# Products of a recommendation tower: one sample on each quarter of the array instead of two on each half

## The chip, the cores and the metric

The kernel runs on one core of a Trainium2 chip. Five engines work side by side, each on its own list of instructions, and wait for each other by semaphores: TensorE (PE: matmuls, with the weight loads, PEld, beside them), VectorE (DVE), ScalarE (ACT), GpSimd (POOL) and SyncE (SP, which here only issues DMAs). Operands lie in SBUF (128 partitions), matmul results in PSUM. The time is that of one execution on the device, in microseconds (us).

## The reference, cut to what matters

```
e = stack([tbl_t[ids[:, t]] for t in range(26)], axis=1)      # 2048 samples, 26 embeddings of 128
combined = concatenate([e, dense[:, None, :]], axis=1)        # 27 features of 128 per sample
interact = einsum('bfd,bgd->bfg', combined, combined)         # 27 x 27 products per sample
z = interact[:, triu_i, triu_j]                               # the 351 pairs above the diagonal
h = concatenate([z, dense], axis=1)                           # 479
h = maximum(h @ W_top1 + b_top1, 0)                           # 512
h = maximum(h @ W_top2 + b_top2, 0)                           # 256
y = h @ W_top3                                                # 1
```

Everything is fp32. Ten of the tables have 1000 rows, the others 1250 to 125000.

## The kernel before

The 2048 samples go through in 8 units of 256. In each unit:

- POOL gathers rows of 16 tables by indirect DMA, one table for 128 samples at a time: 32 gathers (L402), in 8 banks of four. The place `emb` exists once, so a bank's gathers of the next unit may begin when PE has transposed the present ones. PE transposes a bank (L426, four matmuls with the identity) and ACT copies it to `feat` (L588).
- The ten tables of 1000 rows ("held") stay in SBUF, split in a high and a low part (`held_h`, `held_l`). Their rows are picked by matmuls: DVE compares the ids of 256 samples, which a DMA has spread over all partitions (`ids_row`), with row numbers and so makes a one-hot matrix `hot` (L689, two halves of 128 x 1024 per table); PE multiplies it with the table (L440 and L441, 16 matmuls per table). `hot` has two places, so the one-hot of a table waits until the table two before it has been used. `ids_row` has ten.
- PE multiplies each sample's 27 features with each other (L458). Two samples stand side by side as 54 columns, both as weights and as what streams past them, and the result is 54 x 54, of which the two blocks of 27 x 27 on the diagonal are of use. The left half of the array (result rows 0 to 53) has one pair of samples, the right half (rows 64 to 117) the next. A batch is 8 such groups of four samples, 432 columns in a bank of PSUM; a unit has 8 batches. ACT copies each to `gram` (L603).
- SP stores `gram` to DRAM (four DMAs, L323) and, when they have landed, loads the 351 pairs from there in the layout of a matmul operand (15 DMAs, L329). ACT and DVE split them in `z_h` and `z_l`.
- The layers of the unit before (L476 first, L510 and L515 second, L525 the last) are put between the tables and the products of the present one.

The order of the work is a list of steps that all engines walk through (`steps`, L89): each kind of step has a span of the unit, and `merged` sorts them by place. First the four row banks of samples 0 to 127 among the ten tables, then the other four row banks among the first half of the products, then the second half of the products. The first layer of the unit before stands at about 0.62 of the tables' part.

At the start the ids of all gathers are loaded by the ACT queue (L641), before the first two tables; SP loads ids and tables 2 to 9 at the same time. After the last unit's products come the stores, the loads of pairs, and the layers of the last unit.

Of the kernel before, what the change touches and what calls it, by code (L numbers as in the profile page):

```python
# [30 lines left out]
def dlrm_tower_kernel(nc, x_t, ids_g, ids_h, gathered, held, w1, b1, w2, b2, w3, out):  # L31
# [16 lines left out]
    S = 4  # L48
    SIDES = 2
    PAIR = S // SIDES  # L50
# [4 lines left out]
    BANK = 512  # L55
    GB = 8
    BATCHES = UC // S // GB
# [11 lines left out]
    PC = HC // PIECES  # L69
    SLOTS = NH  # L70
    PER_ROW = 2
    AHEAD = 2
    BANKS = [(f, min(4, NG - f)) for f in range(0, NG, 4)]
# [15 lines left out]
    def steps(later, last=False):  # L89
        rows = [("rows", w) for w in range(UNIT * NB)]  # L90
        tables = [("held", o) for o in range(NH)]
        gram = [("gram", b) for b in range(BATCHES)]
        z = [("z", c) for c in range(ZC)] if later else []
        l1 = [("l1", n) for n in range(1 if last else N1)] if later else []
        l2 = [("l2", n) for n in range(N2)] + [("weigh", 0)] if later and not last else []
        l3 = [("l3", 0)] if later and not last else []
        following = [("next hot", (o, q)) for o in range(2) for q in range(PIECES)]

        found = []
        for step in merged((rows[:NB], 0.05, 0.8), (tables, 0, 1), ([("dense", 0)], 0.6, 0.8), (z, 0.58, 0.64),  # L100
                           (l1, 0.9 if last else 0.62, 1)):
# [3 lines left out]
        found += merged((rows[NB:], 0, 1), (gram[:HALF], 0.1, 1), (l2, 0, 0.7), (following[:PIECES], 0, 1))  # L105
        return found + [("parts", 0)] + merged((gram[HALF:], 0, 1), (l3, 0, 0.1), (following[PIECES:], 0, 1))

# [25 lines left out]
    with ctx:  # L133
# [38 lines left out]
        for name, shape, dt in (("z_raw", [ZR, ZC, UC], fp32), ("z_h", [ZR, ZC, UC], f32r), ("z_l", [ZR, ZC, UC], f32r),  # L172
# [3 lines left out]
            late_at += 4 * math.prod(shape[1:])  # L176
        assert late_at <= placed_at["hot"] + 4 * 2 * HC * UC
        held_h = sb("held_h", [HR, NH, HC, D], f32r)
# [31 lines left out]

        ids_in = sem("ids_in")
        rows_in = [[sem(f"rows_in{h}_{w}") for w in range(NB)] for h in range(UNIT)]
        ids_row_in = [sem(f"ids_row_in{p}") for p in range(NH // PER_ROW)]
        dense_in = sem("dense_in")
# [119 lines left out]
        def _(sp):  # L334
# [13 lines left out]
            def load_ids_rows(i, p):  # L348
                reached(sp, hot_made, ((i - 1) * NH + (p + 1) * PER_ROW) * PIECES)
                sp.dma_start(ids_row[:, p * PER_ROW:(p + 1) * PER_ROW, :].rearrange("q o b -> q (o b)"),  # L350
                             ids_h[i:i + 1, p * PER_ROW * UC:(p + 1) * PER_ROW * UC].to_broadcast([128, PER_ROW * UC])
                             ).then_inc(ids_row_in[p], 16)
# [12 lines left out]
            def store_y(j):  # L365
                sp.wait_ge(y_made, j + 1)
                sp.dma_start(out[:, j * UC:(j + 1) * UC], y_of(j)[:]).then_inc(y_out, 16)

            load_ids_rows(0, 0)
            for o in range(AHEAD, NH):  # L370
                if o % PER_ROW == 0:
                    load_ids_rows(0, o // PER_ROW)
                load_table(sp, o)
            load_dense(0)
            for i in range(UNITS):
                if i == 0:
                    weights()
                if not is_last(i):
                    for p in range(NH // PER_ROW):
# [10 lines left out]
        def _(pool):  # L390
# [16 lines left out]

            pool.wait_ge(ids_in, 16)
            for i in range(UNITS):
                gather(i)  # L410

        @block.tensor
        def _(pe):
# [16 lines left out]
            def table(i, o):  # L430
# [6 lines left out]
                for c in range(HC):  # L437
                    if c % PC == 0:
                        pe.wait_ge(hot_made, n * PIECES + c // PC + 1)
                    nc.tensor.matmul(dst, held_h[:, o, c, :], hot[:, n % 2, c, :], start=c == 0, stop=False)  # L440
                    ins = nc.tensor.matmul(dst, held_l[:, o, c, :], hot[:, n % 2, c, :], start=False, stop=c == HC - 1)  # L441
                ins.then_inc(hot_used, 1)
# [123 lines left out]
        def _(act):  # L566
# [56 lines left out]
            def unit(i):  # L623
                for kind, k in steps(i > 0, is_last(i)):
# [9 lines left out]
                    elif kind == "parts":  # L634
                        dense_part(i)
                    elif kind in ("z", "l1", "l2"):
                        later(i - 1, kind, k)
                    elif kind == "hot" and k[1] == 0 and i == 0 and k[0] + 1 < NH:
                        table_high(k[0] + 1)

            act.dma_start(idx[:], ids_g[:, :, :]).then_inc(ids_in, 16)  # L641
# [4 lines left out]
            for o in range(3):  # L646
                table_high(o)
# [20 lines left out]
        def _(dve):  # L668
# [14 lines left out]
            def one_hot(i, o, q):  # L683
                n = i * NH + o
                if q == 0:
                    dve.wait_ge(ids_row_in[o // PER_ROW], 16 * (i + 1))
                    reached(dve, hot_used, n - 1)
                chunks = slice(q * PC, (q + 1) * PC)
                nc.vector.tensor_tensor(hot[:, n % 2, chunks, :],  # L689
                                        bass.AP(ids_row, (n % SLOTS) * UC, [[SLOTS * UC, HR], [0, PC], [1, UC]]),  # L690
                                        row_nums[:, chunks].unsqueeze(2).to_broadcast([HR, PC, UC]),
                                        ALU.is_equal).then_inc(hot_made, 1)
# [63 lines left out]
            def unit(i):  # L756
                for kind, k in steps(i > 0, is_last(i)):
                    if kind == "hot":
                        if i == 0 and k[1] == 0:
                            table_low(k[0])  # L760
                        one_hot(i, *k)
                        if i == 1 and k[1] == PIECES - 1 and k[0] - 2 < NW:
                            weights_low(k[0] - 2)
                    elif kind == "next hot":
# [13 lines left out]
            dve.wait_ge(rows_numbered, 1)  # L778
            for o in range(2):
                for q in range(PIECES):  # L780
# [66 lines left out]
```

## Time and profile before

| | |
|---|---|
| median of 3 runs | 375.73 us (374.99 to 376.73) |
| profiled execution | 375.79 us |
| its span, first to last instruction | 373.8 us |
| mean granted clock of TensorE | 0.977 |
| busy: PE / PEld / DVE / ACT / POOL | 333.4 / 315.3 / 247.8 / 203.4 / 252.8 us |
| products (L458): matmuls in the trace | 2048 |
| HBM read / written | 38.07 / 6.20 MB |

A busy PE is not a PE at its peak: matmuls overlap, so their cost is read from the distance of their starts. The program's fp32 matmuls appear as two each in the trace. Idle time before an instruction is put down to whoever released it. A granted clock of 1.00 is 2.4 GHz, 0.50 is 1.2 GHz.

### The profile page before, as it was taken

The numbers are of one execution on the slowest core, as the hardware profiler recorded it, in microseconds if no ns is written. First come the engines' busy times: TensorE is split into PE (matmuls) and PEld (weight loads), VectorE is DVE, ScalarE is ACT, GpSimd is POOL, SyncE is SP. The second block draws the span as 40 slices with busy tenths as digits, with TensorE's granted clock in tenths as the row PEclk, the third lists the DMA queues.
The fourth block names the chain that finished last, engine by engine and source line by source line (L and its number), as shares of the span: only waits on it lengthen the run. The fifth ranks groups of instructions, "written<-read, shape, count | busy, mean of one in ns | idle before, by whom it ended". The sixth has DMA issues, their size and how long they took to land.

```text
span 373.8 us, 9779 instructions
## 1 busy us (share of the span) xinstructions
PE 333.4 (89%) x4178; PEld 315.3 (84%) x4178; DVE 247.8 (66%) x298; ACT 203.4 (54%) x274; POOL 252.8 (68%) x262
## 2 busy tenths in 40 slices
PE   0768759969999899989999999989998999989967
PEld 0768649869899898989899998989898989988955
DVE  3999805994469835895389735995389645980324
ACT  1575475425756448536755456645855466548322
POOL 3888777877777777777777777777777777760000
PEclk9998979989999999999999999999999999999989
DMA  7995324453154532563254623563255524420310
GB/s 238 392 322 166 97 59 132 107 156 84 51 131 121 162 81 69 155 184 85 53 155 100 175 63 91 143 180 80 56 155 147 136 51 119 113 72 2 87 39 0
DMA packets 32377, 44.92 MB, mean 120 GB/s; under 512 B 18791, under 2 KB 20463, under 8 KB 32334
## 3 DMA queue, kind: packets, MB, share of 16 engines
q1 hardware_dynamic: 23080, 25.82, 24.0%
q0 software_dynamic: 8192, 16.79, 17.6%
q10 hardware_dynamic: 1062, 1.69, 1.4%
q8 instruction: 33, 0.54, 0.6%
q14 instruction: 10, 0.08, 0.1%
HBM read 38.07 MB, written 6.20 MB: 118 GB/s over the span
## 4 chain that ended last, share of the span: by engine, by line
PE 49%; DVE 21%; POOL 10%; issue 8%; DMA 6%; SPq 3%; ACT 2%; ACTq 0%; DVEq 0%
DVE hot L689 18%; PE ps_gram L458 14%; POOL emb L402 10%; PE ps_mix L476 10%; PE ps_feat L440 7%; PE ps_feat L441 7%; PE ps_feat L426 4%; PE ps_mix L510 3%; DMA products_dram<-gram 3%; SPq L329 3%; ACT feat L588 1%; DMA idx<-in_ids 1%; PE ps_mix L515 1%; PE ps_feat L476 1%; PE ps_mix L525 1%
## 5 line engine op out<-in xcount | busy, mean ns | idle before, releaser
L402 POOL DMA_INDIRECT emb<-in_tbl,idx x256 | 252.1, 985 | 81.7 <-issue 76.8
L689 DVE TENSOR_TENSOR hot<-ids_row,ps_rows 128x1024 fp32r<-128x1024 int32 x160 | 186.2, 1215 | 19.1 <-PE ps_feat L441 16.1
L440 PE MATMUL ps_feat<-hot,held_h 128*128 128x256 f32 x640 | 164.8, 295 | 15.5 <-DVE held_l L675 11.7
L588 ACT COPY feat<-ps_feat 128x512 f32<-128x512 f32 x104 | 125.7, 1229 | 76.6 <-PE ps_feat L426 44.5
L441 PE MATMUL ps_feat<-hot,held_l 128*128 128x256 f32 x640 | 159.6, 287 | 0.0
L440 PEld LDWEIGHTS ps_feat<-hot,held_h 128*128 128x128 f32 x640 | 125.0, 195 | 17.8 <-issue 14.8
L441 PEld LDWEIGHTS ps_feat<-hot,held_l 128*128 128x128 f32 x640 | 125.2, 196 | 0.0
L458 PEld LDWEIGHTS ps_gram<-feat 128*54 128x54 f32 x2048 | 56.0, 132 | 9.7 <-issue 5.4
L458 PE MATMUL ps_gram<-feat 128*54 128x54 f32 x2048 | 61.0, 217 | 1.3 <-ACT feat L588 1.3
L426 PE MATMUL ps_feat<-ident,emb 128*128 128x128 f32 x256 | 40.8, 283 | 9.0 <-DMA emb<-in_tbl,idx 9.0
L603 ACT COPY gram<-ps_gram 119x432 f32<-119x432 f32 x64 | 35.2, 550 | 9.6 <-PE ps_gram L458 9.5
L615 ACT ACTIVATE h_h<-ps_mix,b_sb 128x256 fp32r<-128x256 f32 x28 | 13.3, 474 | 49.8 <-DVE h_x L742 49.7
L426 PEld LDWEIGHTS ps_feat<-ident,emb 128*128 128x128 f32 x256 | 29.6, 143 | 10.8 <-issue 9.5
L742 DVE TENSOR_SCALAR h_x<-ps_mix,b_sb 128x256 f32<-128x256 f32 x28 | 13.5, 483 | 32.4 <-PE ps_mix L476 32.4
L476 PE MATMUL ps_mix<-z_h,w1z_h 117*128 117x256 f32 x84 | 24.2, 288 | 5.1 <-DVE z_l L734 5.1
L704 DVE TENSOR_TENSOR den_l<-dense,den_h 128x256 fp32r<-128x256 f32 x7 | 4.5, 639 | 31.4 <-ACT den_h L595 31.4
L476 PE MATMUL ps_mix<-z_l,w1z_h 117*128 117x256 f32 x84 | 23.8, 284 | 0.0
L476 PE MATMUL ps_mix<-z_h,w1z_l 117*128 117x256 f32 x84 | 23.6, 281 | 0.0
L476 PEld LDWEIGHTS ps_mix<-z_h,w1z_h 117*128 117x128 f32 x84 | 15.9, 189 | 6.1 <-DVE z_l L734 6.1
L476 PEld LDWEIGHTS ps_mix<-z_h,w1z_l 117*128 117x128 f32 x84 | 16.1, 191 | 0.0
L476 PEld LDWEIGHTS ps_mix<-z_l,w1z_h 117*128 117x128 f32 x84 | 15.9, 190 | 0.0
L510 PE MATMUL ps_mix<-h_h,w_h 128*128 128x256 f32 x45 | 14.0, 311 | 1.4 <-DVE h_l L727 1.4
(101 smaller groups left out, 248.4 us busy)
## 6 DMA issues: line engine op xcount, KB each, us to landing
ids_row<-in_ids_h SPq DMA_DIRECT2D x40, 256.0 KB, 3.9
products_dram<-gram SPq DMA_DIRECT2D x30, 189.0 KB
held_raw<-in_held SPq DMA_DIRECT2D x8, 512.0 KB, 13.1
emb<-in_tbl,idx POOLq DMA_INDIRECT x256
z_raw<-products_dram SPq DMA_DIRECT2D x84, 26.0 KB
held_raw<-in_held ACTq DMA_DIRECT2D x2, 512.0 KB, 9.2
dense<-in_dense_t SPq DMA_DIRECT2D x8, 128.0 KB
w1z_raw<-in_W_top SPq DMA_DIRECT2D x3, 234.0 KB
```

Of the source, the lines that this page charges most:

```text
L402: pool.indirect_dma_start(emb[:, h, f, :], None, table, bass.IndirectOffsetOnAxis(ap=idx[:, i * UNIT + h, f:f + 1].bitcast(u32), axis=0),) ...
L426: ins = nc.tensor.transpose(ps_feat[:, slot_of(i, ("rows", k)), f * TILE:(f + 1) * TILE], emb[:, h, first + f, :], ident[:])
L440: nc.tensor.matmul(dst, held_h[:, o, c, :], hot[:, n % 2, c, :], start=c == 0, stop=False)
L441: ins = nc.tensor.matmul(dst, held_l[:, o, c, :], hot[:, n % 2, c, :], start=False, stop=c == HC - 1)
L458: ins = nc.tensor.matmul(ps_gram[side * SIDE:side * SIDE + M, nth % GRING, g * M:(g + 1) * M], two, two, start=True, stop=True)
L476: ins = nc.tensor.matmul(bank_of(j, "l1", k), *term, start=c == 0 and m == 0, stop=c == ZC and m == 2)
L510: nc.tensor.matmul(bank_of(j, "l2", k), *term, start=c == 0 and m == 0, stop=False)
L588: nc.scalar.copy(feat_v[:, f, b], src).then_inc(act_out, 1)
L603: nc.scalar.copy(*products_copy(i, b)).then_inc(gram_act, 1)
L615: nc.scalar.activation(h1_h[:, k, :], bank_of(j, kind, k), ACT.Relu, bias=b1_sb[:, k:k + 1]).then_inc(h1_high, 1)
L689: nc.vector.tensor_tensor(hot[:, n % 2, chunks, :], bass.AP(ids_row, (n % SLOTS) * UC, [[SLOTS * UC, HR], [0, PC], [1, UC]]), row_nums[:, ...
L742: nc.vector.tensor_scalar(h1_x[:, k % 2, :], bank_of(j, kind, k), b1_sb[:, k:k + 1], 0.0, ALU.add, ALU.max).then_inc(h1_full, 1)
```

## The change

Three things are changed together.

**Products.** `SIDES` goes from 2 to 4: a matmul has one sample, 27 columns, and writes 27 rows of PSUM from partition 0, 32, 64 or 96 on. There are twice as many. A batch has 16 groups of four samples (`GB`), still 432 columns, so a unit has four batches. `gram` needs 27 x 64 numbers per partition in place of 54 x 64.

**One-hots and ids.** In the room freed, `hot` has three places (`HOTS`); the next unit's first three one-hots are made beside the products, not two. `ids_row` has places for four pairs of tables in place of five, taken in turn; the fifth pair of the next unit is loaded after the stores of the products.

**Start.** The ids for unit 0's gathers are loaded alone, as SP's first DMA; POOL waits for them, and for the others before unit 1. SP waits for table 0 before it issues further loads.

```
-    SIDES = 2
+    SIDES = 4
-    GB = 8
+    GB = 16
-    SLOTS = NH
     PER_ROW = 2
+    ROW_SLOTS = 4
+    HOTS = 3
...
-        following = [("next hot", (o, q)) for o in range(2) for q in range(PIECES)]
+        following = [("next hot", (o, q)) for o in range(HOTS) for q in range(PIECES)]
...
-            if step[0] == "held" and step[1] + 2 < NH:
-                found += [("hot", (step[1] + 2, q)) for q in range(PIECES)]
+            if step[0] == "held" and step[1] + HOTS < NH:
+                found += [("hot", (step[1] + HOTS, q)) for q in range(PIECES)]
...
-        ids_row = sb("ids_row", [128, SLOTS, UC], i32)
-        hot = sb("hot", [HR, 2, HC, UC], f32r)
+        ids_row = sb("ids_row", [128, ROW_SLOTS * PER_ROW, UC], i32)
+        hot = sb("hot", [HR, HOTS, HC, UC], f32r)
...
             def load_ids_rows(i, p):
-                reached(sp, hot_made, ((i - 1) * NH + (p + 1) * PER_ROW) * PIECES)
+                nth = i * (NH // PER_ROW) + p
+                reached(sp, hot_made, (nth - ROW_SLOTS + 1) * PER_ROW * PIECES)
...
+                    for p in range(ROW_SLOTS, NH // PER_ROW):
+                        load_ids_rows(i + 1, p)
                     reached(sp, l2_done, i * N2)
...
+            sp.dma_start(idx[:, 0:UNIT, :], ids_g[:, 0:UNIT, :]).then_inc(first_ids_in, 16)
             load_ids_rows(0, 0)
+
+            sp.wait_ge(held_in[0], 16)
             for o in range(AHEAD, NH):
                 if o % PER_ROW == 0:
                     load_ids_rows(0, o // PER_ROW)
                 load_table(sp, o)
+                if o == AHEAD:
+                    sp.dma_start(idx[:, UNIT:, :], ids_g[:, UNIT:, :]).then_inc(other_ids_in, 16)
...
-            pool.wait_ge(ids_in, 16)
-            for i in range(UNITS):
+            pool.wait_ge(first_ids_in, 16)
+            gather(0)
+            pool.wait_ge(other_ids_in, 16)
+            for i in range(1, UNITS):
                 gather(i)
...
-                    reached(dve, hot_used, n - 1)
+                    nth = n // PER_ROW
+                    dve.wait_ge(ids_row_in[nth % ROW_SLOTS], 16 * (nth // ROW_SLOTS + 1))
+                    reached(dve, hot_used, n - HOTS + 1)
```

The end of a middle unit on PE before, from its third-last row bank on (`rows_in1_1` and on are banks 5 to 7, `ps_gram<-feat` the products, counted as the program's matmuls, 16 in a batch):

```order
436 L426 MATMUL ps_feat<-ident,emb 128x128 [waits rows_in1_1,act_out]
438 L458 MATMUL ps_gram<-feat 54x54 [waits gram_act]
439 L458 MATMUL ps_gram<-feat 54x54 x15
440 L426 MATMUL ps_feat<-ident,emb 128x128 [waits rows_in1_2,act_out]
442 L458 MATMUL ps_gram<-feat 54x54 [waits gram_act]
444 L426 MATMUL ps_feat<-ident,emb 128x128 [waits rows_in1_3,act_out]
446 L458 MATMUL ps_gram<-feat 54x54 [waits gram_act]
448 L525 MATMUL ps_mix<-h_x,ones 1x256 [waits weighed,h2_made]
449 L458 MATMUL ps_gram<-feat 54x54 [waits gram_act,act_out]
```

And the same place after the change:

```order
428 L439 MATMUL ps_feat<-ident,emb 128x128 [waits rows_in1_1,act_out]
430 L439 MATMUL ps_feat<-ident,emb 128x128 [waits rows_in1_2,act_out]
432 L471 MATMUL ps_gram<-feat 27x27 [waits gram_act]
433 L471 MATMUL ps_gram<-feat 27x27 x63
434 L439 MATMUL ps_feat<-ident,emb 128x128 [waits rows_in1_3,act_out]
436 L538 MATMUL ps_mix<-h_x,ones 1x256 [waits weighed,h2_made]
437 L471 MATMUL ps_gram<-feat 27x27 [waits gram_act,act_out]
438 L471 MATMUL ps_gram<-feat 27x27 x63
439 L471 MATMUL ps_gram<-feat 27x27 [waits gram_act]
440 L471 MATMUL ps_gram<-feat 27x27 x63
```

Between banks 5 and 6, and behind bank 7, no batch stands any more; four batches of 64 matmuls take the place of eight of 16.

SP's list at the start of the program, before (`ids_row` a pair of rows of ids, `held_raw` a table):

```order
1 L350 DMA ids_row<-in_ids_h 128x512 x2
2 L315 DMA held_raw<-in_held 128x1024 x2
3 L350 DMA ids_row<-in_ids_h 128x512
4 L315 DMA held_raw<-in_held 128x1024 x2
5 L350 DMA ids_row<-in_ids_h 128x512
```

And after (`idx` are the ids of the gathers):

```order
1 L375 DMA idx<-in_ids 128x32
2 L354 DMA ids_row<-in_ids_h 128x512
3 L354 DMA ids_row<-in_ids_h 128x512 [waits held_in0]
4 L317 DMA held_raw<-in_held 128x1024
5 L384 DMA idx<-in_ids 128x224
6 L317 DMA held_raw<-in_held 128x1024
```

The first ids of the gathers are now SP's first DMA, and all but two of its loads stand behind a wait for table 0. Later, between a unit's stores and its loads of pairs on SP, one load of ids has been put:

```order
47 L325 DMA products_dram<-gram 28x1728 [waits gram_act]
48 L325 DMA products_dram<-gram 28x1728 x3
49 L354 DMA ids_row<-in_ids_h 128x512 [waits hot_made,gram_stored]
50 L331 DMA z_raw<-products_dram 26x4x64 [waits l2_done]
51 L331 DMA z_raw<-products_dram 26x4x64 x3
```

Before, row 49 is not there, and all five loads of ids stand ahead of the stores.

## Rows read from the trace of the kernel before

**Rows 1.** The page: busy us (share of the span) x instructions; unit 2 as a window.
```profile
PE 333.4 (89%) x4178; PEld 315.3 (84%) x4178; DVE 247.8 (66%) x298; ACT 203.4 (54%) x274; POOL 252.8 (68%) x262
...
107.05:148.39 41.34, 40.12 (x524) 38.30 (x523) 28.99 (x36) 23.78 (x32) 31.29 (x34) 1.00 0.44 117
```
**Rows 2.** Chain of waits (start, us, what): last products of units 1 and 2.
```profile
103.68 3.37 PE ps_gram L458 x128
...
145.02 3.37 PE ps_gram L458 x128
```
**Rows 3.** POOL: its gathers (ns min/median/max), three of them in time.
```profile
L402 POOL DMA_INDIRECT emb<-in_tbl,idx x256: 940/944/1853, 5.4 to 334.3; - x128
...
93.80 0.94 POOL L402 DMA_INDIRECT emb<-in_tbl,idx  x1 [0.30 <-issue]
...
133.91 0.95 POOL L402 DMA_INDIRECT emb<-in_tbl,idx  x1 [0.30 <-issue]
...
334.35 0.94 POOL L402 DMA_INDIRECT emb<-in_tbl,idx  x1 [0.30 <-issue]
```
**Rows 4.** Chain of waits, start and unit 0's end; granted clock there.
```profile
0.74 4.41 DMA idx<-in_ids
...
5.42 1.09 POOL emb L402
...
51.58 2.54 DMA emb<-in_tbl,idx
...
54.25 1.09 PE ps_feat L426 x4
55.34 5.20 PE ps_gram L458 x160
...
50.70:57.50 6.80, 4.20 (x76) 3.73 (x72) 0.00 (x0) 3.73 (x7) 5.28 (x6) 0.50 0.22 58
```
**Rows 5.** Durations (ns min/median/max), then in time; products begun by 144.96, 145.06, 145.11.
```profile
L458 PE MATMUL ps_gram<-feat x2048: 213/213/337, 45.3 to 347.6; 128*54 128x54 f32 x187
...
L525 PE MATMUL ps_mix<-h_x,ones x12: 377/377/378, 103.1 to 310.0; 128*1 128x256 f32 x12
...
144.43 0.59 PE L525 MATMUL ps_mix<-h_x,ones 128*1 128x256 f32 x2
...
144.95 0.26 PE L458 MATMUL ps_gram<-feat 128*54 128x54 f32 x2
...
144.95 0.31 PE L458 MATMUL ps_gram<-feat 128*54 128x54 f32 x4
...
144.95 0.36 PE L458 MATMUL ps_gram<-feat 128*54 128x54 f32 x6
```
**Rows 6.** DVE's one-hots in unit 2; then the chain where z arrives.
```profile
105.40 2.34 DVE L689 TENSOR_TENSOR hot<-ids_row,ps_rows 128x1024 fp32r<-128x1024 int32 x2
109.26 13.76 DVE L689 TENSOR_TENSOR hot<-ids_row,ps_rows 128x1024 fp32r<-128x1024 int32 x12 [1.52 <-PE ps_feat L441]
...
122.93 0.43 DVE z_l L734
```
**Rows 7.** The last unit's end: PE's last row bank, and the chain behind it.
```profile
342.28 0.66 PE L426 MATMUL ps_feat<-ident,emb 128*128 128x128 f32 x4
...
343.27 1.09 ACT feat L588
...
344.40 3.46 PE ps_gram L458 x128
...
347.88 0.53 ACT gram L603
```
**Rows 8.** Chain: the last load of pairs of unit 6; the tail by its clock.
```profile
327.62 0.37 SPq L329
...
328.03 1.76 DMA z_raw<-products_dram
...
361.30:364.70 3.40, 3.08 (x14) 3.08 (x15) 1.61 (x5) 0.47 (x1) 0.00 (x0) 0.50 0.00 0
```

More of the change, by code:

```diff
@@ L102, in steps @@
             found.append(step)
-            if step[0] == "held" and step[1] + 2 < NH:
-                found += [("hot", (step[1] + 2, q)) for q in range(PIECES)]
-        found += merged((rows[NB:], 0, 1), (gram[:HALF], 0.1, 1), (l2, 0, 0.7), (following[:PIECES], 0, 1))
-        return found + [("parts", 0)] + merged((gram[HALF:], 0, 1), (l3, 0, 0.1), (following[PIECES:], 0, 1))
+            if step[0] == "held" and step[1] + HOTS < NH:
+                found += [("hot", (step[1] + HOTS, q)) for q in range(PIECES)]
+        found += merged((rows[NB:], 0, 1), (gram[:HALF], 0.1, 1), (l2, 0, 0.7), (following[:HOTS * PIECES // 2], 0, 1))
+        return found + [("parts", 0)] + merged((gram[HALF:], 0, 1), (l3, 0, 0.1), (following[HOTS * PIECES // 2:], 0, 1))
     def is_last(j):
@@ L176, in dlrm_tower_kernel @@
             late_at += 4 * math.prod(shape[1:])
-        assert late_at <= placed_at["hot"] + 4 * 2 * HC * UC
+        assert late_at <= placed_at["hot"] + 4 * HOTS * HC * UC
         held_h = sb("held_h", [HR, NH, HC, D], f32r)
@@ L209, in dlrm_tower_kernel @@
         row_nums = ps_rows[0:HR, 0, 0:HC].bitcast(i32)
-        ids_in = sem("ids_in")
+        first_ids_in = sem("first_ids_in")
+        other_ids_in = sem("other_ids_in")
         rows_in = [[sem(f"rows_in{h}_{w}") for w in range(NB)] for h in range(UNIT)]
-        ids_row_in = [sem(f"ids_row_in{p}") for p in range(NH // PER_ROW)]
+        ids_row_in = [sem(f"ids_row_in{p}") for p in range(ROW_SLOTS)]
         dense_in = sem("dense_in")
@@ L348, in load_ids_rows @@
             def load_ids_rows(i, p):
[L349 to L350 removed]
+                nth = i * (NH // PER_ROW) + p
+                reached(sp, hot_made, (nth - ROW_SLOTS + 1) * PER_ROW * PIECES)
+                slot = nth % ROW_SLOTS * PER_ROW
+                sp.dma_start(ids_row[:, slot:slot + PER_ROW, :].rearrange("q o b -> q (o b)"),
                              ids_h[i:i + 1, p * PER_ROW * UC:(p + 1) * PER_ROW * UC].to_broadcast([128, PER_ROW * UC])
[L352 removed]
+                             ).then_inc(ids_row_in[nth % ROW_SLOTS], 16)
             def products_through_dram(i):
@@ L378, in _ @@
                 if not is_last(i):
-                    for p in range(NH // PER_ROW):
+                    for p in range(ROW_SLOTS):
                         load_ids_rows(i + 1, p)
@@ L439, in table @@
                         pe.wait_ge(hot_made, n * PIECES + c // PC + 1)
-                    nc.tensor.matmul(dst, held_h[:, o, c, :], hot[:, n % 2, c, :], start=c == 0, stop=False)
-                    ins = nc.tensor.matmul(dst, held_l[:, o, c, :], hot[:, n % 2, c, :], start=False, stop=c == HC - 1)
+                    nc.tensor.matmul(dst, held_h[:, o, c, :], hot[:, n % HOTS, c, :], start=c == 0, stop=False)
+                    ins = nc.tensor.matmul(dst, held_l[:, o, c, :], hot[:, n % HOTS, c, :], start=False, stop=c == HC - 1)
                 ins.then_inc(hot_used, 1)
@@ L637, in unit @@
                         later(i - 1, kind, k)
-                    elif kind == "hot" and k[1] == 0 and i == 0 and k[0] + 1 < NH:
-                        table_high(k[0] + 1)
-            act.dma_start(idx[:], ids_g[:, :, :]).then_inc(ids_in, 16)
+                    elif kind == "hot" and k[1] == 0 and i == 0:
+                        table_high(k[0])
             for o in range(AHEAD):
@@ L645, in _ @@
             nc.scalar.copy(h1_x[:, 1, 0:1], ones[:])
-            for o in range(3):
+            for o in range(HOTS):
                 table_high(o)
@@ L761, in unit @@
                         one_hot(i, *k)
-                        if i == 1 and k[1] == PIECES - 1 and k[0] - 2 < NW:
-                            weights_low(k[0] - 2)
+                        if i == 1 and k[1] == PIECES - 1 and k[0] - HOTS < NW:
+                            weights_low(k[0] - HOTS)
                     elif kind == "next hot":
@@ L778, in _ @@
             dve.wait_ge(rows_numbered, 1)
-            for o in range(2):
+            for o in range(HOTS):
                 for q in range(PIECES):
```

6 lines of the change are left out of this document (3 added, 3 removed).

## The prediction

> **What bounds the kernel now.** The busy shares come first: PE is at 89%, POOL at 68% [rows 1]. A middle unit of 256 samples takes 41.34 us from its last product to the next unit's (103.68 + 3.37 = 107.05, then 145.02 + 3.37 = 148.39) [rows 2], and PE shows 40.12 us of busy time in it [rows 1]. So PE is the bound, but POOL is close. Its list shows 256 gathers of 0.944 us, and 0.30 us of idle time before each, which is put down to "issue" and to no other engine [rows 3]. From the last gather of unit 1 (93.80) to that of unit 2 (133.91) it needs 40.11 us for 32, 1.25 each, and waits for nobody [rows 3]. The last one starts at 334.35, and nothing in it depends on PE. Between a gather's start and its landing lie 2.54 us (the last of unit 0: 51.58 to 54.12) [rows 4]; so the last rows of all are there at about 336.9, while PE transposes them at 342.28 [rows 7]. PE is 5.4 us late. That is all that a faster PE can win before POOL becomes the wall, unless POOL itself starts earlier.
>
> **The products, part by part.** A program matmul in fp32 is two matmuls in the trace: 1024 of them stand as 2048 [rows 5]. Per unit there are 256 with 54 columns; now 512 with 27. Do they cost half as much each, or the same? In one batch two have begun by 144.96, four by 145.06, six by 145.11, and the last of each ends 0.26, 0.31 and 0.36 after the start. At 0.213 apiece (0.25 for the first) the second begins at 144.957, the fourth at 145.047, the sixth at 145.097 [rows 5]: two start nearly together, and the next two 50 ns later. The two matmuls on 256 fp32 columns (L525) last 0.59 together and 0.377 each [rows 5], so a stream of 256 takes 0.213 us, and 54 columns 45 ns. The two halves of the array therefore each take 45 + 5 ns per matmul, side by side: 25 ns apiece on average. With 27 columns a quarter takes 22.5 + 5 = 27.5 ns. Four starts, at the spacing seen between two (7 ns by estimate), take 28 ns. I forecast 7 ns apiece: 512 x 7 = 3.6 us per unit, where now 128 take 3.37 [rows 2] and 256 about 6.7. Bounds: as above; or 13.5, if no more than two run at a time (no gain); or 26, if the average of 25 (26.3 with the batch's ends) is a price per instruction and not per column, which doubles the 6.7 to 13.5. I choose the low one, since two start within 10 ns of each other: the engine can hand out a load and a matmul in that time.
>
> The Trainium skill, TensorE: Matmul & The Clock Gate, section "Wait — 56ns, not 53.3ns?", speaks against this: matmuls never start less than about 25 ns apart, however few columns they have. The two starts within 10 ns say that it doesn't hold between column tiles, but the average of 25 ns here is just that figure, so it stays as a rival. The same skill's TensorEngine Tiling (Array Packing), section "Instruction Overhead", puts the overhead at some 60 cycles and warns against taking a tiling factor from a dimension that is already small.
>
> **Copies on ACT.** Batches go from 8 to 4 per unit with the same 432 columns, so four copies of 0.53 go, 2.1 us of ACT per unit; a bank of features still costs 1.1 [rows 7]. This is of use only at the unit's end: after it two row banks stand next to each other, and ACT (1.1 + 1.1 + 0.6 + 1.1, from 0.44 after the first) feeds the last products 4.3 us after the transposes of bank 5, against 5.0 now. Gain 0.7.
>
> **Three places for one-hots.** Now DVE has one table ready, makes the second at 105.40, must wait till 109.26 for a place, and then needs 13.76 us for 12 halves, 1.15 each, 2.3 per table [rows 6], while PE, begun at 107.05, has freed a place by 109.26, 2.2 with hand-over, 1.9 without. The third place takes that stall (some 2.5 us over six tables). But the next thing late is already in the row: PE's first layer waits for z_l, made from 122.93 to 123.36, 16.3 us after the last product of the unit before [rows 6]. That time is the way through DRAM and does not shrink: SP even has one more load (the fifth pair of ids) between the stores and the loads of pairs, 0.4 us of issue. Its wait is for the first two tables of the next unit; DVE makes them beside the last products, before the stores have landed, so it holds nothing up, though all 15 loads of pairs are queued behind it. So PE comes earlier and waits longer; I book nothing for the one-hots and +0.4 for the load. If z were not in the way, it would be -2.5 a unit, and POOL would take it back.
>
> **The unit after.** 41.34 - 0.7 - (3.37 - 1.8) for the last products + 0.4 = 39.5 us for PE, against 40.1 for POOL. POOL becomes the bound, by little.
>
> **The start.** The ids come now as 128 KB on ACT's queue, from 0.74, in 4.41 us; the first gather starts at 5.42 [rows 4]. After, 16 KB go first on SP's queue. The nearest rows are small loads at the end of unit 6: issued at 327.62, there at 329.79, 2.2 us [rows 8]. With 0.27 to the gather this gives 3.3, a gain of 2.1 (bounds 0, where two tables of 512 KB in front of the same engines hold it up, and 2.4). The 8 us that unit 0 takes over 40 (gathers up to 1.85 long [rows 3]) stay, since as many subtractions of tables run beside them. The rest of the ids and tables 2 to 9 now wait until table 0 has landed; unit 1's first gather is 47 us away, table 9 is used near 40, so they are hidden. Without that cover each us late there is one us late in PE's unit 0, which POOL's schedule covers again.
>
> **The sum.** Last rows there: 336.9 - 2.1 = 334.8. Is PE there in time? Unit 0 ends (now 55.34 + 5.20 = 60.55 [rows 4]) with POOL's rows, 2.1 earlier, and with faster products: some 56.5. Unit 1 keeps its 46.5, set by one-hots and weight halves on DVE, less 3: 100, against 107.05. Five units of 40.1 end at 300 to 301; now it is 313.75. The last unit needs 28.5 to bank 7 (now 313.75 to 342.28), so PE is ready at about 328 and waits 6 us for POOL. Then, from the landing: 0.14 to PE, 1.09 for the transposes at the lower clock as in unit 0 [rows 4], ACT's copy 1.1, 256 products, ACT's copy 0.53 [rows 7]. The products cost 1.8 at 7 ns. But in unit 0 PE waited for rows in the same manner, and the granted clock from 50.70 to 57.50 was 0.50, the lower level (1.2 GHz) [rows 4]; there 27 columns take 45 + 3 ns, four quarters 12 apiece, 3.1 us. I take 2.4. Together 334.8 + 0.14 + 1.09 + 1.1 + 2.4 + 0.53 + 0.1 = 340.2, where now it is 348.41 (347.88 + 0.53) [rows 7]. What follows, 25.4 us to the end at 373.8 (stores, loads, two layers), is the same code, and PE is at the lower clock in it already (361.3 to 364.7) [rows 8]. Span 365.6; with the 2.0 us that lie around the span in the profiled run (375.79 - 373.8), 367.6. That run is 0.06 from the median of 375.73. I forecast 367.5.
>
> **Rivals.**
> 1. Quarters don't run more than two at a time (13.5 ns apiece). For it: only two starts together are seen. Against: nothing but columns separates the quarters. The products cost 6.9 as now; unit 0 ends 2 to 3 us earlier by POOL's start, the units gain 0.3 each at most. 375.8 - 2.5 - 1.3 = 372.
> 2. A price per instruction, on the other side. Place: L471, 4096 matmuls. At 26.3 ns apiece a unit's products take 13.5 instead of 6.9: +6.4, eight times 51, less the 3.8 of rival 1: about 423. For it: the average of exactly 25 ns, and that no stretch of the trace shows a shorter average over ten. Against: starts within 10 ns, and then 45 + 5 explained by columns alone. It decides from 13.9 ns + 3.8 / (8 x 0.512) = 14.8 ns apiece; a partial form (say 17 ns, instructions fetched too slowly for batches of 256) gives +9, 385.
> 3. The wait moves and the gain is lost: PE's pauses before banks 5 to 7 (one each 5 us from POOL) drop its clock in every unit, and z comes later by SP's extra load. At half clock for 3.4 us a unit costs 1.7 more: 39.5 + 1.7 = 41.2, nothing gained in the middle; but then there is no pause any more. End: 375.8 - 2 of the start, up to +1: 373 to 377.
>
> **Chances.** Forecast (POOL is the wall) 0.66, 364 to 370.5. Rival 1: 0.12. Rival 2: 0.14. Rival 3: 0.08, most of it within 0.5%, which is 1.9 us and about what a measurement can tell from no change. Faster: 0.66 + 0.12 + 0.01 = 0.79; same 0.06; slower 0.14 + 0.01 = 0.15. The range takes rival 1 and the start's bounds in: 363.5 to 374. Rival 2 stays out.
>
> **What would show it.** L471's batches of 128 in the trace at 0.9 us (forecast), 1.8 (rival 1), 3.3 (rival 2); POOL's first gather at 3.3, its last at 332.2; PE idle before L439 with DMA as releaser in units 3 to 7; PE's wait for z_l near 3 us a unit instead of 1; DVE's wait for a free place gone; last ACT copy ending at 340. I am wrong if PE, not POOL, sets the period of the middle units, or the period is above 40.2.

## The result, and the profile after

The changed kernel takes 397.51 us (median of 5 runs, 392.55 to 397.97), the kernel before 375.73: ratio 1.0569, 95% interval [1.0519, 1.0619]. It is slower by 5.7%; forecast were 367.5, range 363.5 to 374. Run once more on another chip (e9 below) it was 1.0640 [1.0607, 1.0672]. The profiled execution is the fastest of the five, 392.55 us, span 390.7, and its parts are read here. Its mean granted clock is 0.969; the other four have 0.948 to 0.961 and take 397.35 to 397.97 us.

The page of the changed kernel, its columns as in [rows 1] and, for groups, busy us, mean ns of one | idle before them:

```profile
PE 329.4 (84%) x6226; PEld 307.7 (79%) x6226; DVE 248.1 (64%) x298; ACT 187.7 (48%) x242; POOL 253.8 (65%) x262
...
q8 instruction: 49, 0.80, 0.8%
...
L471 PE MATMUL ps_gram<-feat 128*27 128x27 f32 x4096 | 55.1, 197 | 24.2 <-issue 12.4
L471 PEld LDWEIGHTS ps_gram<-feat 128*27 128x27 f32 x4096 | 45.9, 108 | 37.1 <-issue 22.5
```

PE is busy for less time than in [rows 1], 329.4 instead of 333.4, in a span 17 us longer. What grew is idle time ahead of the products, and most of it has "issue" as its releaser: PE waited for nothing that the profile shows. The queue q8 brings instructions. It moved 49 packets, before 33 (0.54 MB). Sixteen more packets of 256 instructions are 4096: just the 2048 weight loads and 2048 matmuls that were added.

The chain of waits at the end of unit 4 (start, us, what), where 103.68 and 145.02 stood in [rows 2]:

```profile
236.12 0.52 ACT gram L616
236.63 1.08 ACT feat L601
...
237.75 0.70 PE ps_gram L471 x49
...
239.22 0.71 PE ps_gram L471 x30
...
240.47 0.41 PE ps_gram L471 x13
240.88 1.22 issue
242.10 0.67 PE ps_gram L471 x47
```

And PE's own list of the same stretch (last: idle before):

```profile
237.75 3.13 PE L471 MATMUL ps_gram<-feat 128*27 128x27 f32 x202 [0.97 <-ACT feat L601]
242.10 0.67 PE L471 MATMUL ps_gram<-feat 128*27 128x27 f32 x54 [1.22 <-issue]
```

The last 256 products of the unit take 5.02 us with their standstill; 128 took 3.37 in [rows 2], and 1.8 to 2.4 were forecast for 256. The starts in the trace, one by one, show two prices. The first 30 of a batch start 7.6 ns apart on average, near the forecast. Over a run of about 55 the mean is some 9 ns, and after each run there is a pause of 0.2 to 0.3 us. A batch of 128 in which nothing is waited for so comes to 1.62 us, 12.8 ns apiece. The second price is the standstill, 0.7 to 2.2 us from start to start in this trace; the last batch of a unit, which has one, takes 2.7 to 3.5 us.

The standstills follow the instructions. PE stops at 240.88 and waits for no semaphore that the profile shows. This is what q8 moved from 239.3 to 240.7 (packets, MB, share); from 238.0 to 239.3 and from 240.7 to 243.1 it moved nothing:

```profile
q8 instruction: 1, 0.02, 5.6%
```

The packet ended at 240.66, and the products went on at 242.10. Counted over the trace, for every distance above 0.5 us between the starts of two products with no other matmul between them: how many of PE's records stand before it in the trace (loads and matmuls, and also its 151 others, nearly all waits for semaphores), and the time from the end of the last q8 packet to the restart.

```
kernel        count before the gap                      restart after packet
changed       1217 4289 4545 5313 6081 7617 9153 ...    1.28 to 1.54 us (10 gaps)
e1            1217 2753 4289 4545 5313 5825 6081 ...    1.24 to 1.62 us (13)
e4            1217 2753 4033 4289 4545 5569 5825 ...    1.25 to 1.54 us (18)
e10            961 1217 2497 2753 4033 4289 4545 ...    1.23 to 1.58 us (19)
```

Every one of these counts is 193 more than a multiple of 256, and so it is in the traces of e3, e5, e7 and e9: 109 gaps in the eight traces with 4096 products, at whatever time they fall. Two packets never begin less than 3.27 us apart in them. So in a sprint PE is fed at most 256 instructions in some 3.3 to 3.9 us. 128 products with their loads are 256 instructions and want to be through in 1.6 us, so PE uses up what was fetched ahead.

The end, against [rows 7]:

```profile
355.42 1.02 PE ps_feat L439 x8
...
359.39 1.17 ACT feat L601
...
360.60 2.69 PE ps_gram L471 x204
363.29 2.02 issue
365.31 0.63 PE ps_gram L471 x43
...
365.96 0.53 ACT gram L616
```

The last copy ends at 366.49 instead of 348.41.

POOL, against [rows 3, 4] (start, us, [idle before]):

```profile
4.16 1.09 POOL L413 DMA_INDIRECT emb<-in_tbl,idx  x1 [2.70 <-DMA idx<-in_ids]
...
335.54 0.94 POOL L413 DMA_INDIRECT emb<-in_tbl,idx  x1 [0.30 <-issue]
```

It starts 1.26 us earlier and begins its last gather 1.2 later than before; it has waited 2.9 us in all for PE (`emb` not yet free), where before it waited 0.9. It is not the wall.

Where the 16.9 us between the two spans lie, from last product to last product: the middle units 2 to 6 take 45.6, 44.4, 43.6, 43.2 and 43.7 us instead of 41.3 each, +13.9; unit 1 49.1 instead of 46.5, +2.6; the last unit 36.2 instead of 34.1, +2.1; unit 0 and the tail -1.7.

Of the 2.8 us that a middle unit takes longer, 1.9 are standstills, and 1.0 is a longer wait of PE for ACT's copy of bank 7 (weight loads of the products, units 2 to 6, before and after):

```profile
PEld ps_gram L458 <- ACT feat L588: 2.2, 5, 0.4
PEld ps_gram L471 <- ACT feat L601: 7.1, 5, 1.5
```

None of it is the clock: units 2 to 6 of this execution ran at 1.00 throughout (window, us, busy of PE, PEld, DVE, ACT, POOL, then granted clock, DMA share, GB/s). That is not so in most of the runs below.

```profile
109.11:329.71 220.60, 198.21 (x3891) 185.63 (x3891) 146.31 (x176) 108.26 (x140) 166.17 (x175) 1.00 0.40 113
```

**What a lower clock costs.** In unit 1 the kernel before and e2 (below) do the same work, and in one of them the clock fell for 3.4 us. These are the two windows of unit 1 and that stretch of the kernel before:

```profile
60.55:107.05 46.50, 42.68 (x523) 40.08 (x523) 32.37 (x42) 23.59 (x32) 35.83 (x36) 0.96 0.40 107
81.40:84.80 3.40, 3.40 (x18) 3.40 (x18) 2.33 (x3) 1.04 (x3) 2.61 (x3) 0.51 0.42 107
59.82:104.79 44.97, 41.14 (x524) 38.53 (x523) 31.84 (x41) 23.50 (x32) 34.59 (x35) 1.00 0.42 109
```

3.4 us at the lower level (1.2 GHz) go with 1.5 us more, 0.45 us for each. In e8 the table matmuls around such a stretch say the same: they follow each other every 0.21 us at 0.50 and every 0.12 us at 1.00.

### The profile page after: what moved, and what is told of

It reads as the page before. It is cut to its first block, busy times and chain, and to the rows that moved or that the text cites. A ratio compares the mean times of both kernels' runs of the same rounds, so it can differ in the third digit from the quotient of the medians.

```text
span 390.7 us, 13845 instructions
## 1 busy us (share of the span) xinstructions
PE 329.4 (84%) x6226; PEld 307.7 (79%) x6226; DVE 248.1 (64%) x298; ACT 187.7 (48%) x242; POOL 253.8 (65%) x262
## 4 chain that ended last, share of the span: by engine, by line
PE 51%; DVE 20%; issue 12%; POOL 9%; ACT 4%; DMA 3%; SPq 0%; ACTq 0%; DVEq 0%; POOLq 0%
DVE hot L702 18%; PE ps_gram L471 13%; POOL emb L413 9%; PE ps_mix L489 9%; PE ps_feat L453 9%; PE ps_feat L454 9%; PE ps_feat L439 4%; PE ps_mix L523 3%; ACT feat L601 2%; PE ps_feat L489 1%; DMA products_dram<-gram 1%; PE ps_mix L528 1%; ACT gram L616 1%; DMA late_z_raw<-products_dram 1%; DMA idx<-in_ids 1%
## 5 line engine op out<-in xcount | busy, mean ns | idle before, releaser
L601 ACT COPY feat<-ps_feat 128x512 f32<-128x512 f32 x104 | 124.2, 1228 | 76.8 <-PE ps_feat L439 43.0
L471 PE MATMUL ps_gram<-feat 128*27 128x27 f32 x4096 | 55.1, 197 | 24.2 <-issue 12.4
L471 PEld LDWEIGHTS ps_gram<-feat 128*27 128x27 f32 x4096 | 45.9, 108 | 37.1 <-issue 22.5
L756 DVE TENSOR_SCALAR h_x<-ps_mix,b_sb 128x256 f32<-128x256 f32 x28 | 13.5, 482 | 53.5 <-PE ps_mix L489 53.5
L439 PE MATMUL ps_feat<-ident,emb 128*128 128x128 f32 x256 | 39.3, 282 | 5.0 <-DMA emb<-in_tbl,idx 5.0
L616 ACT COPY gram<-ps_gram 124x432 f32<-124x432 f32 x32 | 16.8, 524 | 43.9 <-PE ps_gram L471 43.9
```

The lines of the kernel that those rows point to most:

```text
L439: ins = nc.tensor.transpose(ps_feat[:, slot_of(i, ("rows", k)), f * TILE:(f + 1) * TILE], emb[:, h, first + f, :], ident[:])
L471: ins = nc.tensor.matmul(ps_gram[side * SIDE:side * SIDE + M, nth % GRING, g * M:(g + 1) * M], two, two, start=True, stop=True)
L601: nc.scalar.copy(feat_v[:, f, b], src).then_inc(act_out, 1)
L616: nc.scalar.copy(*products_copy(i, b)).then_inc(gram_act, 1)
L756: nc.vector.tensor_scalar(h1_x[:, k % 2, :], bank_of(j, kind, k), b1_sb[:, k:k + 1], 0.0, ALU.add, ALU.max).then_inc(h1_full, 1)
```

## The experiments

The theory, T1: what a product costs is its instructions, both as a rate (12.8 ns per load and matmul) and as a standstill each time a fetched block ends in a sprint. The rivals: the other parts of the change (T2), the coarser batches that let ACT's copy of bank 7 show (T3), the columns. Each ratio is against the kernel before, on the same chip. The times themselves come from several chips, so ratios are the safer comparison between experiments.

**e1, the quarters alone** (the kernel before, with the two constants)

```
-    SIDES = 2
+    SIDES = 4
-    GB = 8
+    GB = 16
```

> The kernel before with the quarters alone (SIDES 4, batches of 16 groups); one-hots, ids and start stay as before. Theory T1 (the engine is supplied with instructions no faster than now, about 12.8 ns per load-and-matmul pair over a batch, and stands still for 1 to 2 us where a sprint of products has used up what was fetched): products cost the same 6.5 us a unit plus 1 to 3 us of standstill; middle units of 43 to 45 us instead of 41.3, time 388 to 396 us. Rival T2 (the loss comes from the other parts of the change, third one-hot place, ids, start): 374 to 378 us.

Measured: 403.71 us, ratio 1.0718 [1.0639, 1.0798]; middle units 45.1 to 46.4 us. The weight loads' waits (us in total, times, longest):

```profile
PEld ps_gram L458 <- issue: 25.7, 55, 2.5
```

The standstills are there, 13 of them, but both the middle units (T1: 43 to 45) and the time (388 to 396) are above T1's ranges. The quarters alone cost 28 us; T2 falls. Part of what is above the range is the clock: units 4 to 6 have 12 us at the lower level, where the changed kernel's profiled execution has none.

**e2, the start alone** (the kernel before, with SP's first loads and POOL's two waits of the change)

> The kernel before with the split load of ids and SP's wait for table 0 alone. T1: not involved; POOL's first gather near 4.2 us instead of 5.4, and since PE sets the pace the time is that of before less what unit 0 gains, 374 to 376 us. Rival T2 (the loss comes in part from the late tables at the start): above 378 us.

Measured: 374.17 us, ratio 0.9959 [0.9933, 0.9986]. POOL's first gather is at 4.19; the middle units stay at 41.33. A small gain, as T1 says.

**e3, two places for one-hots** (the changed kernel with `HOTS = 2`)

> The changed kernel with two places for one-hots (HOTS 2), all else as changed. If the third place costs (in unit 1 the weight halves are bound to one-hots three tables later, 49.2 us there instead of 46.5): 393 to 395 us. If it brings what was meant, removing DVE's wait: 399 to 403. If it is swallowed by the wait for z, as forecast: 397.5 within 1.

Measured: 402.13 us, ratio 1.0682 [1.0628, 1.0736], against 1.0569 [1.0519, 1.0619] and 1.0640 [1.0607, 1.0672] for two measurements of the changed kernel. It doesn't get faster, so the third place does no harm in sum. How much it brings, 2 to 5 us, is not settled: the two measurements of one and the same kernel differ as much. In the two middle units that e3 ran wholly at 1.00 it takes 43.5 and 43.4 us, the changed kernel 43.6 and 43.2 in the same ones; there the place brings nothing.

**e4, batches of 8 groups** (the changed kernel with `GB = 8`)

> The changed kernel with batches of 8 groups (216 columns, 8 batches per unit, so that a batch stands between all row banks and behind bank 7 again). Same number of matmuls. Theory T3 (a good part of the loss is that PE stands still 1.35 us for ACT's copy of bank 7, and that batches of 128 starts are bunched): 386 to 390 us. T1 alone: instructions are as many, the standstills only move, 393 to 398 us.

Measured: 407.61 us, ratio 1.0848 [1.0772, 1.0923]: neither range. T3 falls; finer batches are worse. The chain of its unit 4:

```profile
246.91 0.34 PE ps_gram L471 x10
247.25 1.72 issue
248.97 1.19 PE ps_gram L471 x74
...
250.99 1.43 issue
```

With a batch always at hand PE pauses less for ACT and more for instructions: 3 to 5 us of standstill in each of units 2 to 6, where the changed kernel has 1.3 to 2.8. And its clock falls behind them: units 2 to 6 have a granted clock of 0.94 and 28.8 us at the lower level, in the changed kernel's profile 1.00 and none. Those units take 233.6 us instead of 220.6. The weight loads of the products wait 9.3 us more there for instructions and 5.8 less for ACT's copies. That leaves 9.5 us of the 13.0, which is 0.33 for each us at the lower level by this reckoning. So T1's account (the waits move) and a lower clock together cover e4's time. No run sets the clock apart, so this is read from the traces and not tested.

**e5, 13 of 27 columns** (half of each product matrix is not computed)

```
-  ins = nc.tensor.matmul(ps_gram[..., g * M:(g + 1) * M], two, two, ...)
+  ins = nc.tensor.matmul(ps_gram[..., g * M:g * M + 13], two, two[:, 0:13], ...)
```

> The changed kernel with only 13 of the 27 columns streamed per product matmul (half of each product matrix is not computed); instructions as many, weights loaded as before. Columns theory (the 12.8 ns per pair is the time of 27 columns on a quarter of the array): steps within batches fall towards half, products from 6.5 to 4 us a unit, 380 us or less. T1 (supply of instructions): steps and standstills as in the changed kernel, 393 to 399 us.

Measured: 403.25 us, ratio 1.0728 [1.0656, 1.0800]. Its matmuls and its standstill (ns min/median/max; then the chain):

```profile
L471 PE MATMUL ps_gram<-feat x4096: 173/186/224, 44.9 to 380.9; 128*27 128x13 f32 x196
```

```profile
205.12 0.34 PE ps_gram L471 x10
205.46 1.85 issue
207.31 0.64 PE ps_gram L471 x27
```

Half the columns streamed, and no time saved: product to product, without the standstills, a unit's steps sum to 6.2 to 7.1 us, in the changed kernel to 6.4 to 6.9. The columns theory falls for the streamed side; the weights kept their 27 columns. The time is above the range given (393 to 399); its four runs lie between 400.1 and 408.5, and the profiled one is the slowest, at a mean clock of 0.924.

**e6, every second product left out** (sides 1 and 3 are not computed)

```
-                    for side in range(SIDES):
+                    for side in range(0, SIDES, 2):
```

> The changed kernel with every second product matmul left out (sides 1 and 3 are not computed): 256 starts a unit as before the change, 27 columns each. T1: the standstills inside the products vanish, steps sum to 3.3 us a unit at 12.8 ns each or less, PE needs less than POOL, and the middle units take POOL's 40.1 us; 366 to 371 us. If the price is not in the number of instructions but in the quarters themselves (switching between them): above 378 us.

Measured: 370.31 us, ratio 0.9855 [0.9802, 0.9909]. The products (ns min/median/max), then the chain of waits in a middle unit:

```profile
L471 PE MATMUL ps_gram<-feat x2048: 185/188/248, 44.0 to 344.4; 128*27 128x27 f32 x187
```

```profile
224.35 0.94 POOL emb L413
225.29 0.30 issue
```

The chain of waits now runs through POOL's gathers. Not one standstill above 0.35 us is left between products; the middle units take 39.7 to 40.9 us, POOL's pace. This is the clearest test of the standstills: the same batches and order, half the instructions, and 27 us less. It also shows that what was forecast behind the products is there: with cheap products POOL is the wall, at about the time forecast.

On the rate it contradicts T1. Its 64 products of a batch start 14.0 ns apart without any pause, not at 12.8 or less. Only two of the four quarters are used here, so each takes a product every 28 ns, which is the prediction's 27.5 for 27 columns on a quarter. Two quarters so take all that their columns allow, and four do not (12.8 instead of 7).

**e7, weight halves earlier** (the changed kernel)

```
+                        if i == 1 and k[1] == 0 and k[0] - HOTS < NW:
+                            weights_low(k[0] - HOTS)
                         one_hot(i, *k)
-                        if i == 1 and k[1] == PIECES - 1 and k[0] - HOTS < NW:
-                            weights_low(k[0] - HOTS)
```

> The changed kernel with the six subtractions of weights in unit 1 put ahead of the one-hots of tables 3 to 8 instead of behind them. If the longer unit 1 (49.2 against 46.5 us) comes from there, the first of them fills DVE's 4.6 us wait for a place and unit 1 gets 1 to 3 us shorter: 395 to 396.5 us. If not: 397.5 within 1.

Measured: 402.54 us, ratio 1.0641 [1.0577, 1.0705]; unit 1 takes 49.7 us. One subtraction moves into DVE's wait (4.6 us in the changed kernel, 3.1 now), and nothing comes of it. A miss: what makes unit 1 longer is not only where the weights are split. The trace of the changed kernel has another cause: in unit 1 its clock is at the lower level for 7.4 us, before for 3.4. At 0.45 us each that is 1.8 of the 2.6 us by estimate, and the weight loads wait 0.8 us longer there for ACT's copy.

**e8, halves with five places** (products as before, start and lead as changed; the larger `gram` leaves room for five halves of one-hots, and ids for three pairs)

```
-    SIDES = 4
+    SIDES = 2
-    GB = 16
+    GB = 8
-    ROW_SLOTS = 4
+    ROW_SLOTS = 3
+    PLACES = 5
...
-        hot = sb("hot", [HR, HOTS, HC, UC], f32r)
+        hot = sb("hot", [HR, PLACES, PC, UC], f32r)
```

> Products on halves as before (54 columns, 256 starts a unit), with the start of the changed kernel and a longer lead for one-hots: five places for half one-hots instead of four (three whole ones don't fit beside the larger gram), ids in three places for pairs. T1: no standstills, and the longer lead brings part of the 1.2 us a unit that lie between PE's 41.3 and POOL's 40.1: 366 to 373 us, below the start alone (374.2). If the lead is worth nothing without quarters: 374 within 1.

Measured: 389.61 us, ratio 1.0399 [1.0354, 1.0445]: a miss, and slower by 15 us than the start alone. Middle units take 44.2 us. Chain of its unit 3, and PE's wait:

```profile
204.66 3.95 DMA ids_row<-in_ids_h
...
212.03 2.75 DVE hot L704 x3
214.78 0.64 issue
215.43 0.43 DVE z_l L750
215.90 1.77 PE ps_mix L490 x9
```

```profile
PE ps_mix L490 <- DVE z_l L750: 12.0, 5, 2.7
```

The ids for the fourth and fifth pair come only behind the stores, and DVE waits for them (0.5 us). And a longer lead puts one more table ahead of z on DVE's list: 13 halves of one-hots, not 12, stand between the first free place and z_l. The longer lead is spent there, and PE waits 2.4 a unit for z_l where it waited 1.0.

These 1.4 us are half of what the middle units lose. The other half is the clock: 3.4 us at the lower level are 1.5 at the 0.45 from above. In each of units 2 to 6 it falls for 3.4 us right behind PE's wait for z_l; the one of unit 4 and the stretch behind it:

```profile
216.60:220.00 3.40, 3.40 (x18) 3.40 (x17) 1.05 (x1) 0.00 (x0) 2.48 (x4) 0.50 0.23 60
220.00:223.40 3.40, 3.40 (x31) 3.40 (x30) 2.09 (x4) 0.59 (x2) 2.49 (x4) 1.00 0.19 51
```

18 matmuls against 31. In the kernel before, with 1.0 us of waiting, the clock stays at 1.00 in units 2 to 6.

**e9, the changed kernel again**

> The changed kernel itself once more, beside e10 on the same chip, since kernels with quarters differ by some us from run to run and chip to chip: 395 to 403 us under every theory. Standstills of 1 us and more should again follow the same matmuls by count (T1: the boundary of a fetched block), whatever their time.

Measured: 399.78 us, ratio 1.0640 [1.0607, 1.0672]. All 13 standstills above 0.5 us lie again at 193 past a multiple of 256. Units 2 to 6 take 226.2 us where the first profile has 220.6, and 8.0 us of them are at the lower clock.

**e10, row banks earlier** (the changed kernel)

```
-        found += merged((rows[NB:], 0, 1), (gram[:HALF], 0.1, 1), ...
+        found += merged((rows[NB:], 0, 0.7), (gram[:HALF], 0.1, 1), ...
```

> The changed kernel with the last four row banks put at 0 to 0.7 of the unit's end instead of 0 to 1, so that a batch of products stands behind bank 7 and covers ACT's copy, as before the change. If the 1.35 us that PE waits for that copy are a loss of their own: the middle units lose 1.35 us, 9 us in all against e9. T1, in which the end of a unit is bound by how fast its 1150 instructions are fetched (about 3.7 us for 256): the wait turns into standstill, and e10 is within 4 us of e9.

Measured: 408.98 us, ratio 1.0876 [1.0844, 1.0908]. The waits of e9, then of e10:

```profile
PEld ps_gram L471 <- issue: 24.5, 56, 2.3
PEld ps_gram L471 <- ACT feat L601: 12.8, 9, 1.7
```

```profile
PEld ps_gram L471 <- issue: 39.3, 56, 2.6
```

All but 1.4 of the 12.8 us of waiting for ACT's copy are gone, and 14.8 us of waiting for instructions have come. So the wait for ACT was no loss of its own; it gave the fetch time to catch up. T1's mechanism holds, its number does not: e10 is 9 us slower than e9, not within 4. The rest goes with the clock. Units 2 to 6 of e9, then of e10:

```profile
110.50:336.65 226.15, 201.49 (x3891) 188.76 (x3891) 145.71 (x176) 108.05 (x140) 166.79 (x173) 0.98 0.41 110
111.90:345.43 233.53, 205.76 (x3891) 196.79 (x3891) 145.11 (x175) 107.99 (x140) 164.37 (x173) 0.94 0.40 106
```

8.0 us at the lower level became 28.7. In these units the two waits above come to 2.0 us more, the time to 7.4; what is left, 5.4, is 0.26 for each us more at the lower level. That is less than 0.45, and in part of these stretches PE stands still anyway: in unit 3 of e10 it stands for 1.47 us until 204.38 and for 1.92 until 208.10, and the clock is at 0.50 from 207.4 to 214.2. That the standing still is what lowers it is the likely reading and was not tested.

**e11, halves, and z on two queues** (e2, with ACT issuing 5 of the 15 loads of pairs at table 3, and the splits of z one table earlier)

```
-                           (z, 0.58, 0.64),
+                           (z, 0.49, 0.545),
...
+                        if k == 3 and i > 0:
+                            act.wait_ge(gram_stored, i * S * 16)
+                            reached(act, l2_done, (i - 1) * N2)
+                            load_pairs(act, i - 1, slice(None), (2,))
```

> The halves (products as before), the start of the changed kernel, and z earlier: ACT issues 5 of the 15 loads of pairs, and the splits of z stand one table earlier on ACT and DVE. The quarters' 12.8 ns per pair are not involved. If z_l is late both by SP's issues and by its place behind the one-hots: PE's wait of 1.3 us a unit goes, the middle units come to POOL's 40.1, and the time to 366 to 369 us. If DVE's one-hots alone set the pace: 373 to 375.

Measured: 371.25 us (6 runs), ratio 0.9875 [0.9845, 0.9904]: faster than both kernels, and above the range given by 2 us. A middle unit by its window; DVE around z; and all that POOL waited for PE:

```profile
188.28:228.81 40.53, 40.33 (x524) 38.35 (x523) 28.96 (x36) 23.35 (x33) 30.78 (x33) 1.00 0.44 117
```

```profile
201.66 0.75 DVE L745 TENSOR_TENSOR z_l<-z_raw,z_h 117x256 fp32r<-117x256 f32 x2
203.30 0.43 DVE L745 TENSOR_TENSOR z_l<-z_raw,z_h 117x256 fp32r<-117x256 f32 x1 [0.89 <-ACT z_h L620]
```

```profile
POOL emb L408 <- PE ps_feat L434: 0.3, 1, 0.3
```

PE's wait for z_l has left its list, and the middle units take 40.1 to 40.7 us instead of 41.3, POOL's pace. Two things were changed for z, the second queue and the earlier place; which of them did it was not separated.

## Why the prediction was wrong, point by point

- **What bounds the kernel.** Right: PE by little, POOL right behind it at 40.1 us. e6 and e11 take what is above, and stop there.
- **The products.** This step failed. "I forecast 7 ns apiece" was mis-sized: 12.8 ns over a batch that waits for nothing. The reason given, that two start within 10 ns of each other, was true and told nothing of a sustained rate: the first 30 starts do come at 7.6 ns and a run of 55 at some 9, and then PE pauses. That 12.8 is half of the 25 of before is chance as far as any run shows. So 512 of them cost 6.5 us, as 256 did (6.4), and the expected 3 us a unit went nowhere. This much is near rival 1's number (13.5), but not for its reason: with 9 ns in a run more than two quarters work at a time, and e5 shows that half of the streamed columns change nothing. Whether the 12.8 is a price of instructions, as T1 has it, is not shown: the weight loads kept their 27 columns in e5, and e6 used only two of the quarters.
- **The partial form of rival 2, "instructions fetched too slowly for batches of 256".** This is what came, and it was given a part of 0.14 and 385 us. The prediction took the supply of instructions as free in its sum; the standstills add 1.3 to 2.8 us in units 2 to 6, 1.9 on average. The units take 44.1 on average, 4.6 more than the 39.5 forecast: 1.9 of standstill, 1.6 that the last products were to gain and did not, 1.7 for ACT's copies (1.0 lost, 0.7 expected), less the 0.4 booked for the load of ids, since the wait for z_l grew by 0.1 only. That is 4.8. The number is not that of the partial form (17 ns a product, 385 us), which had neither the copies nor the clock.
- **Rival 2 in full** (26 ns apiece, 423 us) did not come, though the one batch in four that meets the end of a fetched block takes 2.7 to 3.5 us, near its 3.3. (By its own terms its sum should have 6.6 us a unit in place of 6.4, 425 us.) Of the Trainium skill's 25 ns between starts (TensorE: Matmul & The Clock Gate, "Wait — 56ns, not 53.3ns?") the trace shows that it doesn't hold between quarters: some 9 in runs, 12.8 over a batch.
- **Rival 3, the clock falls in PE's pauses** (0.08, 373 to 377 us). In the profiled execution it did not happen in units 2 to 6. In e9, the same kernel, it did: 8.0 us there are at the lower level, in e10 and e4 nearly 29, and each us costs 0.26 to 0.45 by the reckonings above, against the rival's 1.7 for 3.4. The pauses are not those before banks 5 to 7 that the rival named, but lie among and behind the last products. It comes on top of the standstills, and the median's 5 us above the profiled run go with it: the other four runs have the lower mean clocks.
- **ACT's copies, gain 0.7 a unit.** Wrong in sign: PE waits about 1.4 us for the copy of bank 7 (7.1 us in units 2 to 6), before 0.4. But e10 shows that taking it away gains nothing while the supply is short.
- **Three places for one-hots, booked at nothing.** Not contradicted by e3, whose gain of 2 to 5 us lies within what the kernel varies. The wait for z_l, forecast near 3 us, stayed at 1.1, since PE never came earlier. The cause given was incomplete: z_l is late by DRAM, and also by its place on DVE's list. In the changed kernel it stands behind six halves and starts when they end:

```profile
251.87 6.87 DVE L702 TENSOR_TENSOR hot<-ids_row,ps_rows 128x1024 fp32r<-128x1024 int32 x6
258.66 1.09 DVE L748 TENSOR_TENSOR z_l<-z_raw,z_h 117x256 fp32r<-117x256 f32 x3
```

- **Unit 1, which "keeps its 46.5", less 3,** took 49.1, and e7 didn't find the reason. By the traces 4.0 us more at the lower clock are some 1.8 of it, and ACT's copy 0.8. The 46.5 itself held 1.5 us of lower clock, as e2's 45.0 shows.
- **The start, gain 2.1.** Measured 1.26 at POOL (4.16 for 5.42), and 0.4% alone in e2, since PE is the bound. The load of 16 KB took 3.14 us (0.74 to 3.88), not the 2.2 taken over from the small loads of unit 6.
- **The mark of being wrong**, "the period is above 40.2", was met: 43.2 and more. PE, not POOL, set it.

## What to carry to other kernels

Count the instructions of a sprint, not only its columns: splitting matmuls into smaller ones that run side by side is free only while the engine's instructions arrive as fast. From the kernel before, the distance of two starts says how fast the array can take work, not how fast it is fed; read the rate over hundreds. When a stage waits both for data and for instructions, taking the data wait away can just move it. And before a remainder is called open, read the granted clock in the same stages of both runs: here 20 to 29 us more at the lower level were some 5 to 10 us of time.

## What was not expected of the hardware

- PE's instructions come in packets of 16 KB (256 instructions). In a sprint the packets of q8 begin 3.3 to 3.9 us apart, each takes about 1 us, and PE resumes 1.2 to 1.6 us after one has ended. The kernel before, with 256 instructions in its last 3.37 us of a unit, stays clear of this. It has one gap above 0.5 us between two products, 0.73 us in the last unit, and there PE waits for ACT's copy:

```profile
344.40 1.81 PE L458 MATMUL ps_gram<-feat 128*54 128x54 f32 x64 [0.52 <-ACT feat L588]
```

- On four quarters the first 30 pairs of weight load and matmul of a batch start 7.6 ns apart on average, a run of some 55 has a mean of about 9 ns, and then 0.2 to 0.3 us pass without any. What ends such a run was not found.
- Kernels with 4096 products vary more: the changed one took 392.6 to 398.0 us on one chip and 399.4 to 401.7 on another, where the kernel before stayed within 372.4 to 378.6 on all. The time goes with the mean granted clock: 0.969 for the run of 392.6, 0.948 to 0.961 for the other four on that chip. In the profiled runs the clock falls around the last products of a unit, in none of units 2 to 6 in one run and in all of them in another (e10).
